# Attention values in DRAM by store unit instead of by head: one 8 KB run per store, four 512-byte runs per load

## What is computed

```python
k = split_heads(ctx @ Wk + bk)          # 16 heads x 4096 keys x 16
v = split_heads(ctx @ Wv + bv)          # 16 heads x 4096 keys x 16
scores = q k^T / sqrt(16), masked in layers 0 and 1
attn = softmax(scores)                  # layer 0: times group_prob
x = x + (attn @ v) @ Wo + bo
```

## Time and profile before

| | |
|---|---|
| median of 3 runs | 1538.91 us (1538.9 to 1542.71) |
| profiled execution, its own time | 1537.95 us |
| profiled execution, span first to last instruction | 1536.7 us |
| PE busy | 1420.2 us, 92% |
| DVE busy | 980.9 us, 64% |
| ACT busy | 760.1 us, 49% |
| POOL busy | 526.1 us, 34% |
| first stage | from 0 to about 252 us |
| mean granted TensorE clock | 0.968 |

### The profile page before, as it was taken

The page is one execution under the profiler, slowest core; times in us unless marked ns, Lnnn a source line. Parts: engine busy times, 40 slices in busy tenths (PEclk is TensorE's granted clock), DMA queues, the critical chain, the costliest instruction groups (busy, mean ns, idle before and its releaser), DMA issues. The chain is left out here.

```text
span 1536.7 us, 29870 instructions
## 1 busy us (share of the span) xinstructions
PE 1420.2 (92%) x11216; PEld 838.7 (55%) x11216; DVE 980.9 (64%) x2274; ACT 760.1 (49%) x1020; POOL 526.1 (34%) x638
## 2 busy tenths in 40 slices
PE   8999997999999998799999888699999896999987
PEld 3765753555555555545555555335555583555555
DVE  4444445888888863587878334288886235888842
ACT  5144140444444433168888733247777221777762
POOL 4565242566666650365555522011111001011100
PEclk9999997999999997889999999989999998999999
DMA  8888994244444308235567074536668521476800
GB/s 269 272 273 258 283 287 147 42 67 66 66 65 66 104 2 124 52 49 87 84 94 172 1 195 117 173 63 110 102 100 224 85 39 45 80 108 94 159 8 7
DMA packets 131657, 178.21 MB, mean 116 GB/s; under 512 B 14365, under 2 KB 105525, under 8 KB 124342
## 3 DMA queue, kind: packets, MB, share of 16 engines
q1 hardware_dynamic: 117610, 160.90, 49.2%
q10 hardware_dynamic: 13904, 15.41, 3.1%
HBM read 132.44 MB, written 43.78 MB: 115 GB/s over the span
## 5 line engine op out<-in xcount | busy, mean ns | idle before, releaser
L894 ACT ACTIVATE prob_a<-ps 128x1024 f32<-128x1024 f32 x464 | 456.2, 1023 | 268.1 <-PE ps L768 170.7
L907 DVE CUSTOM_DVE_ANT_0 dump_a<-ps,neg_q 128x512 bf16<-128x512 f32 (+1 forms) x485 | 329.8, 718 | 89.2 <-PE ps L748 87.2
L748 PE MATMUL ps<-kop,qop 116*128 116x512 bf16 x1024 | 343.8, 405 | 38.0 <-DMA qop<-qparts 22.7
L911 DVE TENSOR_REDUCE best_a<-ps 128x1 f32<-128x512 f32 (+1 forms) x488 | 318.6, 709 | 48.5 <-PE ps L748 48.0
L765 PE MATMUL ps<-qop,kop 116*128 116x256 bf16 x2048 | 343.8, 274 | 3.2 <-ACT prob_a L894 2.6
L765 PEld LDWEIGHTS ps<-qop,kop 116*128 116x128 bf16 x2048 | 194.5, 98 | 128.0 <-ACT prob_a L894 12.9
L792 PE MATMUL ps<-prob_a,vop_a 128*32 128x256 f32 x3072 | 191.7, 383 | 3.1 <-POOL prob_a L1026 2.2
L748 PEld LDWEIGHTS ps<-kop,qop 116*128 116x128 bf16 x1024 | 90.1, 102 | 177.2 <-issue 79.5
L1007 POOL TENSOR_TENSOR used_a<-prob_a,gT 128x1024 f32<-128x1024 f32 x64 | 151.6, 2368 | 87.4 <-DVE used_a L924 67.3
L768 PE MATMUL ps<-neg_k,identb 128*128 128x512 bf16 x416 | 159.0, 382 | 0.0
L986 POOL CAST mpart_a<-nmax_a 128x2 bf16<-128x2 f32 x64 | 25.3, 396 | 369.4 <-DVE nmax_a L916 369.4
(11 more groups left out here) (318 smaller groups left out, 1511.7 us busy)
## 6 DMA issues: line engine op xcount, KB each, us to landing
kop<-kparts SPq DMA_DIRECT2D x448, 128.0 KB, 5.0
kparts<-kp SPq DMA_DIRECT2D x64, 384.0 KB, 4.7
vals<-vst SPq DMA_DIRECT2D x16, 1024.0 KB, 6.9
vraw<-vals SPq DMA_DIRECT2D x64, 256.0 KB, 6.4
e_w<-in_e_w SPq DMA_DIRECT2D x4, 2048.0 KB, 11.4
z_w<-in_z_w SPq DMA_DIRECT2D x24, 256.0 KB, 6.9
ctxT<-in_ctxT SPq DMA_DIRECT2D x8, 512.0 KB, 7.8
raw<-in_mask ACTq DMA_DIRECT2D x16, 256.0 KB, 5.7
```

The source lines that it names most:

```text
L748: return pe.matmul(out, qop[0:R_ALL, h, t * P:(t + 1) * P], kop[0:R_ALL, h % UNROLL, j * CHUNK:(j + 1) * CHUNK], start=True, stop=True)
L894: act.activation(prob[:, n % NP, :], st_bank(n), ACT.Exp).then_inc(S("exp_done"), 1)
L907: dve.tensor_tensor_reduce(out=dump[:, k % 2, 0:width], in0=bank, in1=c.neg_q[:, t, j * CHUNK:j * CHUNK + width], scale=1.0, scalar=-3.0e3 ...
L911: dve.tensor_reduce(out, bank, AX.X, ALU.max).then_inc(sem, 1)
```

## The change

The four store units of a layer become the outer order of `vals`: unit n, head, key tile within the unit, channel. A unit's store then writes one run of 8 KB per partition. A head's load reads four runs of 512 bytes per partition, 8 KB apart, and writes them as one run of 2 KB into `vraw`, which holds what it held before. A constant `V_UNITS = 4` names the number of units, the number of slots of `vst` gets the name `VSLOTS` (it stays 2), and the waits are written with it; their values are the same.

```diff
+V_UNITS = 4
...
-            eng.dma_start(self.vraw[:, u, :], self.c.vals[l, :, KT * HD * h:KT * HD * (h + 1)])\
+            eng.dma_start(self.vraw[:, u, :].rearrange("p (n x) -> p n x", n=V_UNITS),
+                          self.c.vals[l, :, :].rearrange("p (n h x) -> p n h x", n=V_UNITS, h=H)[:, :, h, :])\
...
-    VB = 8
-    NV = KT // VB
+    NV, VSLOTS = V_UNITS, 2
+    VB = KT // NV
...
+    units_by = lambda slot, u: 16 * len([i for i in range(u) if i % VSLOTS == slot])
...
-        vst = sb("vst", [P, 2, H, VB, HD], F32)
+        vst = sb("vst", [P, VSLOTS, H, VB, HD], F32)
...
-        vout = c.vals.rearrange("l p (h k e) -> l p h k e", h=H, k=KT)
+        vout = c.vals.rearrange("l p (n h k e) -> l p n h k e", n=NV, h=H, k=VB)
...
-                    sp.dma_start(vout[l, :, :, n * VB:(n + 1) * VB, :], vst[:, b % 2, :, :, :])\
-                      .then_inc(S(f"v_stored{b % 2}"), 16)
+                    sp.dma_start(vout[l, :, n, :, :, :], vst[:, b % VSLOTS, :, :, :])\
+                      .then_inc(S(f"v_stored{b % VSLOTS}"), 16)
...
-                    if k % VB == 0 and b >= 2:
-                        dve.wait_ge(S(f"v_stored{b % 2}"), 16 * (b // 2))
+                    if k % VB == 0 and b >= VSLOTS:
+                        dve.wait_ge(S(f"v_stored{b % VSLOTS}"), 16 * (b // VSLOTS))
```

More of the change, by code:

```diff
@@ L419, in _ @@
                         sp.wait_ge(S(f"k_stored{slot}"), stored_by(slot, NK))
-                    for i in range(2):
-                        sp.wait_ge(S(f"v_stored{i}"), 16 * (NV // 2))
+                    for slot in range(VSLOTS):
+                        sp.wait_ge(S(f"v_stored{slot}"), units_by(slot, NV))
                     sp.wait_ge(S("kop_ones"), UNROLL)
@@ L424, in _ @@
                 sp.wait_ge(S(f"k_stored{slot}"), stored_by(slot, NK * LAYERS))
-            for i in range(2):
-                sp.wait_ge(S(f"v_stored{i}"), 16 * (NV // 2) * LAYERS)
+            for slot in range(VSLOTS):
+                sp.wait_ge(S(f"v_stored{slot}"), units_by(slot, NV * LAYERS))
             sp.wait_ge(S("g_loaded"), 16 * LAYERS)
@@ L547, in _ @@
                     dve.wait_ge(S("v_psum"), v + 1)
-                    if k % VB == 0 and b >= 2:
-                        dve.wait_ge(S(f"v_stored{b % 2}"), 16 * (b // 2))
-                    dve.tensor_tensor(vst[:, b % 2, :, k % VB, :],
+                    if k % VB == 0 and b >= VSLOTS:
+                        dve.wait_ge(S(f"v_stored{b % VSLOTS}"), 16 * (b // VSLOTS))
+                    dve.tensor_tensor(vst[:, b % VSLOTS, :, k % VB, :],
                                       c.ps[:, V_BANKS[v % 4], 0:D].rearrange("p (h e) -> p h e", h=H),
```

## The result

In 22 runs each, beside each other, the changed kernel took 1536.9 us in the median and the kernel before 1541.71. The ratio is 0.9964, with a 95% interval of 0.9951 to 0.9977: 0.36% faster, 5.5 us of 1541.7 (3.5 to 7.6). The forecast was 5.5 us less. In absolute terms it was 1533.4 us, from a kernel before at 1538.91 in three runs; here that kernel took 1541.71. So 1536.9 lies in the stated range (1530.0 to 1539.5) but outside its likeliest case (1531.4 to 1535.4), and it is the difference that came out as forecast. Whether the gain is above the 0.3% of the prediction stays open, since the interval has 0.23 to 0.49%.

What follows compares the result with a forecast made beforehand. PE was taken to bound the kernel, busy 1420.2 of 1536.7 us, with DMA able to bind in the first stage. Terms -4.8, -1.0 and +0.3 summed to -5.5 us: 1533.4 against the median, range 1530.0 to 1539.5.

Steps and rivals of the forecast that it cites:

- The cover and the stops before third units: First stage, layers 0, 2, 3: PE loses DVE's store wait beyond 2.5 us; quicker stores save 4.8 us.
- Turns on the engines: DMA engines alternate queues packet by packet, so 8 KB packets give a layer's first store a larger share beside ACT's loads.
- The last store: End of the first stage: the very last vals store lands 1.0 us earlier and the stage's end gains that.
- The fifth tiles: PE's stops at a layer's fifth value tile come from kparts stores; vals stores have no part; layer 3 3.0 to 3.3 us.
- sign of being wrong: First stores still landing after 9 to 10 us, a value loop beginning with a longer stop, or the end awaiting masks.
- The loads: vraw loads among kparts stores in layers 2 and 3: 0.25 us more each, together +0.3 us, mainly layer 3's first.
- The sum: Whole kernel: third units -4.8, last store -1.0, loads +0.3, giving -5.5 us.
- What gave way: ACT's gT and POOL's masks pay for quicker stores; 3 us of room stay before the stage's end, cost nothing.
- The clock: Half rate after PE's idle at the first stage's end expected as before; 2 us either way, also at later idle places.
- (B): Rival for the stores: gain only by their own packets, -1.6 to -3.9 us, 1535 to 1537.5 with loads; chance 0.30.
- (C): Rival for layers 2 and 3: four 512-byte-run loads at the price per packet, +8.0 us, 1541.1; chance 0.09.
- (D): Rival for the first stage: masks, gT and kparts stores give way, kparts stops shorten too, 1529.5 us; chance 0.13.

Runs made afterwards that it cites:

- e5: Kernel before, old layout, with the 1 MB gT load issued after a layer's sixth mask piece instead of the second; ratio 0.9984 of the kernel before.
- e8: The kernel before itself, run and profiled again as a control; ratio 0.9996.
- e1: Changed kernel with the loads of the kernel before, so only the stores are new; ratio 0.9974 of the kernel before.
- e2: Kernel before with the changed kernel's loads, stores still in 512-byte runs; ratio 0.9989 of the kernel before.
- e9: Changed kernel with the four vraw loads of layers 2 and 3 moved from among the key stores to behind value stores; ratio 0.9946 of the kernel before.
- e11: Changed kernel with both moves, gT late and the four vraw loads behind value stores; ratio 0.9933 of the kernel before.
- e3: Changed kernel with a unit's values in four groups of four heads, so stores write 2 KB runs; ratio 0.9979 of the kernel before.
- e6: Changed kernel with eight store units per layer and four slots, stores in 4 KB runs, loads in 256-byte runs; ratio 0.9969 of the kernel before.
- e7: The changed kernel itself, run and profiled again; ratio 0.9965 of the kernel before.
- e10: Changed kernel with eight store units and the gT load issued late; ratio 0.9973 of the kernel before.
- e4: Changed kernel with the 1 MB gT load issued after a layer's sixth mask piece instead of the second; ratio 0.9965 of the kernel before.
- e12: Kernel before, old layout, with both moves, gT late and the four vraw loads behind value stores; ratio 0.9945 of the kernel before.

## Why the prediction was right, point by point

**The cover and the stops before third units.** Right in the mechanism: DVE's wait beyond 2.5 us is what PE loses, in seven of seven pairs, and no kernel with 8 KB stores has such a stop. The size was taken from the one profile in which all three were whole. Over the three profiles with stores of 512 bytes and the order of before it is 4.8, 3.9 and 2.1, by the mean 3.6 us. e5, which takes away these stops on the old layout, gained 2.5 us (0.3 to 4.6).

**Turns on the engines.** Borne out by the landings: first stores land 1.2 to 3.0 us earlier than before by the means of three profiles each, and `gT` later by 0.7 to 2.1. The turns themselves are not seen in any view. The Trainium skill's rule (DMA: Bandwidth & Descriptors, "Queues, rings and completion order") has each engine go round between its queues by packets. The landings agree with it if a longer run is a longer packet; with shares by bytes I would not expect a later `gT`.

**The last store.** The term was -1.0 and it measured -1.4 (6.50 to 5.08 us in PE's stop). It was mis-sized: 8 KB packets move 416 GB/s, more than the 406 of the fastest loads, and SP issues the store in 0.33 us instead of 0.51. These two make about 0.2 of the 0.4 us; the rest is not explained.

**The fifth tiles.** This is the step that failed: "a `vals` store has no part in that". Against the same loads, stores of longer runs go with fifth-tile stops of layers 2 and 3 that are 1.6 us longer together, and with longer waits of ACT for `kparts` slots. Layer 2's stop, 1.72 us before and 1.42 in e8, became 2.63 and 2.75; it met the prediction's own sign of being wrong. Layer 3's, for which 3.0 to 3.3 us was forecast, was 2.91 and 3.06 (2.99 before, 2.02 in e8). The path from the store to these waits stays open.

**The loads.** The term was +0.3, and the stops show no more: 5.54 and 5.81 us in layers 2 and 3 for the changed kernel against 5.46 in e1, and 4.10 in e2 between the 4.71 and 3.44 of before. In the time e2's interval bounds it by 1.2 us. But the reading under it, that only the first load of layer 3 counts, does not fit e9: with all four out, layer 2's stop fell as well (0.8 to 1.0 us, and 1.3 to 1.5 in layer 3). The 2.2 to 2.4 us together are near four whole transfers at 406 GB/s (2.6 us), so each load may go through to PE, and the 0.25 us more of each would then be up to 1.0. That is argued from e9 and not measured by itself.

**The sum.** The terms as the profiles show them, means of before, e2 and e8 against changed and e7: third units -3.6, last store -1.4, fifth tiles +1.4 (of it +1.6 in layers 2 and 3), or -3.6 us of stops in all. Measured were -5.5 us (3.5 to 7.6). So the 5.5 of the forecast is in part luck: its largest term was taken from the one profile where it was largest, a term of the other sign was missing, and some 2 us of the measured gain are seen in no stop. They may lie in the interval's width or outside the first stage; no profile shows where.

**What gave way.** Right: POOL ended its last mask piece at 245.9 us and the next stage began at 250.4, with 4 us of room. So the end of the stage does not wait for the masks.

**The clock.** I had looked for it at the stage's end only. It also falls at the stops of the fifth tiles, in seven of the fourteen profiles.

**The rivals.** (B) is refuted in its mechanism, since the stops are gone; its times, 1.6 to 3.9 us less, touch the interval of 3.5 to 7.6 only at its edge. The figure of the Trainium skill under (B), 512 bytes as the size from which line rate is reached (DMA: Bandwidth & Descriptors, "Specifications"), does not hold for these stores, 290 against 416 GB/s. (C) is refuted by e2. (D) did not happen: the stops at the fifth tiles did not shorten, they grew.

## What to carry to other kernels

When a buffer's slot waits for a store, ask first what stands beside and ahead of that store: delaying a load that nobody needs soon (e5) took the same stops away as the new layout did. By the landings here, run lengths bear on the share of two queues as well as on the speed of one, so put long runs on the side that something waits for. Moving four small loads out of the one stretch where ACT waits for stores gained 2.9, 4.9 and 6.0 us in three pairs, about as much as the layout change; the fastest kernel (e11) has all three. And take a wait's size from more than one profile: the stops before third units were 4.8, 3.9 and 2.1 us with the same stores.

## What the hardware showed that I had not expected

A stop of PE of 2.0 to 3.5 us within the value tiles was followed, in seven of the fourteen profiles (changed, e2, e3, e6, e7, e8, e10), by a stretch at half rate that cost 1.5 to 2.9 us in the matmuls behind it. In the first profile of the kernel before, with stops up to 2.99 us, it was not, nor in e1, e4 and e5. In the three kernels with the shortest fifth-tile stops in sum (e9, e11, e12) it was not either, and over all their 25 runs the mean granted clock was 0.969 against 0.967 in the other kernels' 124. The length of one stop does not decide it: 2.02 us were followed by half rate in e8, 2.99 in the kernel before were not. So a stop can cost more than its length.

Single profiles of one kernel differ by 4 us of span: 1536.7 and 1540.4 for before, 1539.1 and 1543.0 for the changed one. In the kernel before all of it arose behind the first stage, which ended at the same time in both (next stage from 252.25 and 252.16 us), since shorter stops and half rate offset each other there. In the changed kernel 2.7 us arose in the first stage and 1.2 behind it.

SP's issue of a `vals` store took 0.33 us as 128 runs and 0.51 as 2048, and that of a `vraw` load 0.52 us as 512 runs and 0.42 as 128.
